# A message pass with one fp32 product per tile and a gather ring of 32 groups

## The chip, the cores and the metric

The kernel runs on one core of a Trainium2 chip. The time is the device time of one execution in microseconds; the figures below are the median of three runs and the times of one profiled execution. TensorE (PE) multiplies matrices, VectorE (DVE) and ScalarE (ACT) work on elements, GpSimd (POOL) issues the gathers, and SyncE (SP) issues loads and counts semaphores. All five run programs of their own and meet at semaphores.

## The reference

A graph of 6250 nodes with 96 features and 206,250 edges, sorted by destination. First a message layer, then three attention layers:

```python
def _mlp(h, W, b, gamma, beta):
    h = relu(h @ W + b)
    mu = mean(h, axis=0); var = mean(square(h - mu), axis=0)
    return gamma * (h - mu) * rsqrt(var + EPS) + beta

node_feat = _mlp(x, W_node, ...)                     # 6250 x 96
edge_feat = _mlp(edge_attr, W_edge, ...)             # 206250 x 4 -> 96
message = concatenate([x[row], x[col], edge_feat], axis=1)
message = _mlp(message, W_msg, ...)                  # 206250 x 288 -> 96
agg = segment_sum(message, col)
x = layernorm(x + agg + node_feat)
for l in range(3):                                   # 4 heads of 24
    h = x @ W[l]; e = leaky_relu(alpha_s[src] + alpha_d[dst])
    alpha = softmax of e over the edges of each dst
    x = relu(segment_sum(h[src] * alpha, dst) + bias[l])
x = layernorm(x0 + x)                                # x0: x before the attention
```

## The kernel before

The message product is split by the three parts of its input. `x @ W1` is computed once per node and written to a table in DRAM (`table_m`, 96 wide); the part of the source node is then one gathered row per edge. `x @ W2` belongs to the destination, and since the edges are sorted, a window of 32 destination nodes (`WA`) serves many edges. `edge_feat @ W3` is computed per edge, after the statistics of the edge features are known.

Edges come in 231 groups of 896 (`GE`), seven tiles (`TPG`) of 128. Where a group reaches over the border of a window it needs two steps; a list of steps in DRAM (`steps`), made by the kernel itself, says for each pair of steps which group, window and ring slot they take. The engines load a few values of that list into registers at the head of each pair.

The program goes through these stages, each a block with a barrier behind it:

1. Preparation: the edge attributes are split into bf16 parts and written to DRAM (`edge_parts`), the tables and the list of steps are made. VectorE splits `x @ W2` into three bf16 parts (`b_dram`), which are loaded again as `b_stack`.
2. Edge statistics: 403 chunks of 512 edges, TensorE (L592) to ScalarE's relu (L632) to VectorE's `bn_stats` (L677). GpSimd waits for the tables, clears memory and gathers the first two groups (L626), and then has nothing to do.
3. A small block that clears memory.
4. The message pass (`edge_block` with the class `Message`). It begins with the node products (TensorE L889, VectorE L898). Then each step runs, with lags of one and two steps: TensorE's `edge_product` (L1013: twice `pick`, which lays the digits of the destinations out, and twice `We_b`, the edge features); VectorE's `match_turned` (L924, a 96 x 896 match of destinations against the window's nodes, and the window's rows of b, L930 and L933); ScalarE's `edge_relu` (L986); TensorE's `message_product` (seven times an fp32 product with `W3s`, L1029, and a bf16 product of the match with `b_win`, L1030, into the same sum); VectorE's `add_source` (L953 twice, which adds the gathered rows, and L962), ScalarE's `square` (L993), VectorE's `add_squares` (L917), TensorE's `node_sums` (L1038), VectorE's `accumulate` (L911) and `match` (L940, L944).
5. A closing stage for the sums of the message layer (from L1337 on), then three attention passes through the same `edge_block`, with `table_a`.

GpSimd's order of work is `gather`: for each group it waits until the group's indices are there, until a slot of the ring of eight is free (`freed`), and, from group 8 on, until TensorE has finished the edge product of the same number of steps (`steps_told`, here `u_ready`; L785). Then it issues seven gathers of 128 rows (L790). SyncE hands over: it waits for the loads of edges (`tell_edges`) and for the landing of a group's seven gathers (`hand_over`, L732) and raises the counts that the other engines wait for; `release` (L734) reads when a group's last step is done, waits for it, raises `freed` and loads the edges of the group that takes the slot.

## Time and profile before

| | |
|---|---|
| median of three runs | 10644.16 us (10643.23 to 10644.27) |
| profiled execution | 10621.61 us, span 10619.8 us |
| GpSimd busy | 6506.8 us, 61% of the span |
| TensorE busy | 6152.5 us, 58% |
| VectorE busy | 4582.6 us, 43% |
| ScalarE busy | 3539.3 us, 33% |
| gathers of the message pass (L790, `table_m`) | 1603, 1608.5 us busy, 905.2 us idle before them |
| gathers of the attention passes (L790, `table_a`) | 4851, 4797.2 us busy, 2646.5 us idle before them |

The profile is read from the program's stages to the single step. The busy times are averages over stages with different limits. Idle time is put down to what ended it: "remote" is a semaphore that SyncE, a DMA or another sequencer raised, "issue" is time in which the engine waited for nothing that the profile shows (loading registers counts here), and a name is the instruction that released it. PEclk is the granted clock of TensorE as a share of 2.4 GHz, so 0.50 is 1.2 GHz.

### The profile page before, as it was taken

To read this page: it belongs to the slowest core of one execution; us is meant where nothing else is said; L and a number is where in the kernel's file an instruction comes from. 1 tells how busy PE (TensorE), PEld (TensorE's weight loads), DVE (VectorE), ACT (ScalarE), POOL (GpSimd) and SP (SyncE) were. 2 spreads that over 40 slices of the span, in tenths; PEclk is the share of its full clock that TensorE was granted. 3 is DMA by queue.
4 is the path that set the end of the run, shared out by engine and by line. 5 is a ranking of instruction groups with operands and counts; after the bars stand their busy time and mean duration, and the time that the engine had idled before them with its cause. 6 is when DMAs were issued, how large, how long until landed. Compare 5 with 4: busy or idle time off the path is not lost. (4 is left out here: it accounts for less than half of the span.)

```text
span 10619.8 us, 135368 instructions
## 1 busy us (share of the span) xinstructions
PE 6152.5 (58%) x29838; PEld 5414.6 (51%) x29838; DVE 4582.6 (43%) x11874; ACT 3539.3 (33%) x7369; POOL 6506.8 (61%) x6535
## 2 busy tenths in 40 slices
PE   6777777777855555555545555555454555555553
PEld 2366666666644444444444444444444444444443
DVE  8644444444543333333343333333334333333335
ACT  5411111111133333333333333333333333333333
POOL 0166666666656666666656666666665666666665
PEclk6555555555566666666666666666666666666665
DMA  5111111111111111111111111111111111111111
GB/s 140 27 37 37 36 37 37 37 37 37 35 35 34 34 34 34 34 34 35 34 35 34 35 34 35 34 35 34 34 34 36 34 34 34 35 34 35 34 35 29
DMA packets 310442, 395.85 MB, mean 37 GB/s; under 512 B 196635, under 2 KB 204177, under 8 KB 308201
## 3 DMA queue, kind: packets, MB, share of 16 engines
q0 software_dynamic: 206976, 330.75, 15.3%
q1 hardware_dynamic: 101577, 61.83, 2.6%
q10 hardware_dynamic: 1840, 2.78, 0.1%
q14 instruction: 37, 0.30, 0.0%
q8 instruction: 12, 0.20, 0.0%
HBM read 368.10 MB, written 26.82 MB: 37 GB/s over the span
## 5 line engine op out<-in xcount | busy, mean ns | idle before, releaser
L790 POOL DMA_INDIRECT rows<-table_a,idx x4851 | 4797.2, 989 | 2646.5 <-issue 1608.0
L1241 PE MATMUL ps<-ident,work 128*128 128x128 f32 x4872 | 1182.2, 418 | 2613.5 <-issue 2534.5
L1241 PEld LDWEIGHTS ps<-ident,work 128*128 128x128 f32 x4872 | 948.7, 221 | 2700.8 <-issue 2600.7
L1258 PE MATMUL ps<-rows,work 128*128 x9744 | 1759.6, 351 | 943.3 <-ACT work L1190 756.7
L1258 PEld LDWEIGHTS ps<-rows,work 128*128 128x128 f32 x9744 | 1637.2, 261 | 1128.9 <-issue 1125.0
L790 POOL DMA_INDIRECT rows<-table_m,idx x1603 | 1608.5, 1003 | 905.2 <-issue 522.4
L1197 ACT ACTIVATE work<-work,small 128x896 f32<-128x896 f32 x696 | 725.0, 1042 | 3640.9 <-issue 2316.9
L1134 DVE SCALAR_TENSOR_TENSOR work<-dstf,big,select 128x224 f32 x696 | 314.4, 452 | 3163.7 <-SPq L732 1658.0
L1123 DVE CUSTOM_DVE_ANT_0 work<-work,ps 128x896 f32<-128x896 f32 x696 | 757.0, 1088 | 1229.7 <-issue 924.7
L1029 PE MATMUL ps<-W3s,work 97*128 97x96 f32 x3248 | 1015.7, 468 | 349.4 <-DVE work L953 318.6
L1029 PEld LDWEIGHTS ps<-W3s,work 97*128 97x128 f32 x3248 | 909.7, 330 | 522.2 <-issue 274.8
L1249 PE MATMUL ps<-ident,work 128*128 128x128 f32 x4872 | 1102.1, 398 | 102.2 <-issue 102.2
L1249 PEld LDWEIGHTS ps<-ident,work 128*128 128x128 f32 x4872 | 991.0, 219 | 105.2 <-issue 105.2
L1190 ACT ACTIVATE work<-ps 128x896 f32<-128x896 f32 x696 | 632.0, 908 | 924.0 <-issue 881.4
L993 ACT ACTIVATE work<-work 128x672 f32<-128x672 f32 x232 | 177.5, 765 | 1900.6 <-DVE work L917 1252.2
L1144 DVE TENSOR_TENSOR work<-work,rows 128x896 f32<-128x896 f32 x696 | 761.1, 1093 | 99.2
L1183 ACT ACTIVATE work<-ps,small 128x896 f32<-128x896 f32 x696 | 687.2, 987 | 28.6 <-PE ps L1249 28.6
L1038 PE MATMUL ps<-work 128*97 128x32 f32 x3248 | 571.1, 348 | 5.7 <-issue 5.7
L1038 PEld LDWEIGHTS ps<-work 128*97 128x97 f32 x3248 | 558.6, 285 | 4.3 <-issue 3.5
L953 DVE TENSOR_TENSOR work<-ps,rows 128x384 f32<-128x384 f32 x464 | 220.7, 504 | 612.1 <-remote 538.0
L924 DVE TENSOR_SCALAR work<-ps,base_w,select 96x896 bf16<-96x896 f32 x232 | 279.7, 1206 | 454.1 <-issue 419.4
L1030 PE MATMUL ps<-work 96*128 96x96 bf16 x1624 | 464.9, 286 | 1.0 <-issue 1.0
(256 smaller groups left out, 6042.6 us busy)
## 6 DMA issues: line engine op xcount, KB each, us to landing
rows<-table_a,idx POOLq DMA_INDIRECT x4851
rows<-table_m,idx POOLq DMA_INDIRECT x1617
big<-edge_parts SPq DMA_DIRECT2D x231, 45.5 KB
edge_parts<-big SPq DMA_DIRECT2D x6, 1617.0 KB, 11.7
work<-edge_parts SPq DMA_DIRECT2D x50, 192.0 KB
table_a<-work SPq DMA_DIRECT2D x12, 606.0 KB, 6.4
b_dram<-big SPq DMA_DIRECT2D x3, 1176.0 KB, 8.2
big<-b_dram SPq DMA_DIRECT2D x3, 1176.0 KB
```

What stands on the lines that cost most here:

```text
L790: pool.indirect_dma_start(rows[:, k % RING, j, 0:width], None, table, bass.IndirectOffsetOnAxis(ap=idx[:, k // CHUNK, at:at + 1], axis=0)) ...
L1029: pe.matmul(o, ut[:, j, :], W3s[:], start=True, stop=False)
L1030: last = pe.matmul(o, match[:, j, :], b_win[:, par], start=False, stop=True)
L1038: last = pe.matmul(ps[0:MW, 6 + par, 0:WA], rr[:, par, j, :], eq[:, par, j, :], start=(j == 0), stop=(j == TPG - 1))
L1123: dve.tensor_tensor_reduce(out=logit[:, par], in0=logit[:, par], in1=ps[:, 2 * par:2 * par + 2, :].rearrange("p b n -> p (b n)")[:, 0:GE], ...
L1144: dve.tensor_tensor(masked[:, par], pen.unsqueeze(2).broadcast_to([P, TPG, H, WA]), source, ALU.add).then_inc(s["a_ready"], 1)
L1183: nc.scalar.activation(logit[:, par], ps[:, 2 * par:2 * par + 2, :].rearrange("p b n -> p (b n)")[:, 0:GE], ACT.Relu, bias=alone[:, par:pa ...
L1190: nc.scalar.activation(probT[:, par].rearrange("p j n -> p (j n)"), ps[:, 4:6, :].rearrange("p b n -> p (b n)")[:, 0:GE], ACT.Copy).then_i ...
L1197: nc.scalar.activation(prob[:, par].rearrange("p j e -> p (j e)"), logit[:, par], ACT.Exp, bias=shift[:, par:par + 1]).then_inc(s["p_ready ...
L1241: last = pe.transpose(ps[:, 4 + j // 4, (j % 4) * P:(j % 4 + 1) * P], prob[:, par, j, :], ident[:])
L1249: last = pe.transpose(ps[:, 2 * par + j // 4, (j % 4) * P:(j % 4 + 1) * P], masked[:, par, j].rearrange("p h n -> p (h n)"), ident[:])
L1258: last = pe.matmul(ps[:, 6 + par, 0:D + 1], probT[:, par, j, :], rows_of(at("slot", 3))[:, j, 0:D + 1], start=(j == 0), stop=(j == TPG - 1))
```

## The change

The message pass moves into the block of the edge statistics, and its ring has 32 groups of its own layout (`store`, 7 x 96 columns a group). GpSimd starts to gather when `table_m` is written, 32 groups straight away, beside the edge statistics; from then on a group waits for a free slot, for its indices, and for the landing of the group 16 before it, and no longer for TensorE. The semaphore count `begun` goes, in the attention passes too.

The message product becomes one fp32 product per tile, of depth 128: rows 0 to 95 are the relu of the edge features, rows 96 to 127 the match of the destinations against the 32 nodes of the window, and the weights are `W3` scaled, over the window's 32 rows of b. So `pick` and `We_b` become one matrix `We_dst` of 128 columns (two matmuls instead of four, in banks that alternate), the match is 32 x 896, and the bf16 parts of b with their split, their two window operations and the products L1030 go. The rows of b (`table_b`, fp32 in DRAM) and the edges are loaded by ScalarE, two DMAs per step, two steps ahead. The sums are kept in `XT`, cleared by VectorE before the first step. VectorE reads three quads of the list instead of four, TensorE none instead of one, ScalarE one instead of none. SyncE first issues the chunk loads of the edge statistics and then goes through its `hand_over` and `release`.

```diff
 RING = 8
-ERING = RING
+RING_M = 32
+TOLD_M = 16
+IDX_M = 4
 LAG = 4
-LEAD_M = 0
+LAG_M = 28
...
             @block.gpsimd
             def _(pool):
-                pool.wait_ge(s_tab, 16)
-                pool.wait_ge(shared["idx0"], 16)
-                pool.wait_ge(s_sent_b, 16 * 3)
-                pool.memset(acc_m[:, ESTAT:], 0.0)
-                for g in range(AHEAD):
+                def gather(g, k, turn):
+                    if k % CHUNK == 0:
+                        pool.wait_ge(s_midx[k // CHUNK], turn * 16 + 16)
+                    if not (isinstance(turn, int) and turn == 0 and k < TOLD_M):
+                        pool.wait_ge(shared[f"gat{k % TOLD_M}"], (turn * (RING_M // TOLD_M) + k // TOLD_M) * (16 * TPG))
+                        pool.sem_inc(shared["paced"], 1)
+                    for j in range(TPG):
+                        at = k % CHUNK * TPG + j
+                        pool.indirect_dma_start(store[:, (k * TPG + j) * D:(k * TPG + j + 1) * D], None, table_m,
+                                                bass.IndirectOffsetOnAxis(ap=idx[:, k // CHUNK, at:at + 1], axis=0)).then_inc(shared[f"gat{k % TOLD_M}"], 16)
+
+                pool.wait_ge(s_tab, 16)
+                for g in range(RING_M):
+                    if g == 8:
+                        pool.wait_ge(s_parts, 16 * (len(PARTS) + 2))
+                    if g == 12:
+                        pool.wait_ge(s_tab_b, 16 * 2)
+                    gather(g, g, 0)
+                def gather_later(i, k):
+                    pool.wait_ge(shared["freed"], i * RING_M + (k - (RING_M - 1)))
+                    gather(None, k, i)
...
-                        if not (isinstance(g, int) and g < emit.paced_from):
-                            pool.wait_ge(emit.steps_told, g - emit.lead)
-                            pool.sem_inc(paced, 1)
-                        pool.sem_inc(begun, 1)
...
+                def edge_product(q, par):
+                    pe.wait_ge(s_edges[par], q * 8 + (16 - 8 * par))
+                    if not (isinstance(q, int) and q < 2):
+                        pe.wait_ge(s["ut_ready"], q - 1)
+                        pe.wait_ge(s["eqt_ready"], q - 1)
+                    for half in range(2):
+                        last = pe.matmul(bank(2 * par + half, P, GE // 2), wt["We_dst"][:],
+                                         edges_in[:, par, half * (GE // 2):(half + 1) * (GE // 2)], start=True, stop=True)
+                    last.then_inc(s["u_ready"], 1)
...
+                        for j in range(j0, j1):
+                            last = pe.matmul(ps[:, 4 + half, (j - j0) * D:(j - j0 + 1) * D], both_parts[:, j, :], weights[:, par],
+                                             start=True, stop=True)
...
-                    dve.tensor_scalar(eqT[:, par].rearrange("p (b n) -> p b n", b=2), ps[0:3 * WA, 0:2, 0:GE // 2],
+                    dve.tensor_scalar(uT[D:, par].rearrange("p (b n) -> p b n", b=2), ps[D:, 2 * par:2 * par + 2, 0:GE // 2],
...
+                    dve.wait_ge(s_bin[par], q * 8 + (16 - 8 * par))
+                    dve.tensor_tensor(weights[D:, par], b_in[:, par], bias_b, ALU.add).then_inc(s["win_ready"], 1)
...
+                def step(q, par, live, at):
+                    if live(0):
+                        edge_relu(q, par)
+                    if live(-2):
+                        load_edges(par, at("edges", -2))
+                    if live(1):
+                        square(q - 1, (par - 1) % 2)
+                    if live(-2):
+                        act.wait_ge(s["win_ready"], q + 1)
+                        load_b(par, at("node", -2))
...
+                for g in range(LAG_M):
+                    hand_over(g % TOLD_M, g // TOLD_M)
+                    if g % CHUNK == CHUNK - 1:
+                        load_indices(g // CHUNK + IDX_M, g // CHUNK)
+                LOOPS = (NG - LAG_M - RING_M) // RING_M
+                with sp.Fori(0, LOOPS) as i:
+                    for u in range(RING_M):
+                        k = LAG_M + u
+                        hand_over(k % TOLD_M, i * (RING_M // TOLD_M) + k // TOLD_M)
+                        if k % CHUNK == CHUNK - 1:
+                            load_indices(i * IDX_M + k // CHUNK + IDX_M, k // CHUNK % IDX_M)
+                        release(sp, i * RING_M + u)
...
+                dve.memset(XT[:], 0.0).then_inc(s_clear, 1)
```

The order of GpSimd's instructions at the start of the message gathers, before. `big` is the memory of the sums, `rows` the ring.

```order
L622 MEMSET big 97x3872 [waits s_sent_b,idx0,s_tab]
L626 DMA rows<-table_m,idx 128x96 x14
L553 UNCONDITIONAL_BRANCH
L1051 UNCONDITIONAL_BRANCH [waits barrier_Pool_Activation_PE_DVE_SP_gather]
L1053 MEMSET big 97x2432
L1050 UNCONDITIONAL_BRANCH
L777 UNCONDITIONAL_BRANCH [waits barrier_Pool_Activation_PE_DVE_SP_gather]
L790 DMA rows<-table_m,idx 128x96 x42
L790 DMA rows<-table_m,idx 128x96 [waits u_ready,idx1,freed]
L790 DMA rows<-table_m,idx 128x96 x6
L790 DMA rows<-table_m,idx 128x96 [waits freed,u_ready]
```

The same place now; `store` holds the ring.

```order
L766 UNCONDITIONAL_BRANCH [waits barrier_Pool_Activation_PE_DVE_SP_gather]
L776 DMA store<-table_m,idx 128x96 [waits s_midx0,s_tab]
L776 DMA store<-table_m,idx 128x96 x55
L776 DMA store<-table_m,idx 128x96 [waits s_midx1,s_parts]
L776 DMA store<-table_m,idx 128x96 x27
L776 DMA store<-table_m,idx 128x96 [waits s_tab_b]
L776 DMA store<-table_m,idx 128x96 x27
L776 DMA store<-table_m,idx 128x96 [waits s_midx2,gat0]
L776 DMA store<-table_m,idx 128x96 x6
L776 DMA store<-table_m,idx 128x96 [waits gat1]
```

Two barriers stood between the first fourteen gathers and the rest, and `u_ready` before each group from the ninth on; now 224 gathers follow one barrier, with waits for landings (`gat`) alone from the seventeenth group on.

TensorE, the beginning of a step in the loop of the message pass, before; the pair of L1029 and L1030 stands seven times there, and seven L1038 follow.

```order
L1009 REGISTER_ALU [waits edged]
L1013 ISA [waits eqt_ready,ut_ready]
L1013 MATMUL ps<-big,pick 96x448
L1013 ISA
L1013 MATMUL ps<-big,pick 96x448
L1013 MATMUL ps<-big,sWe_b 96x448 x2
L1024 REGISTER_ALU [waits win_ready,ut_ready,eqt_ready]
L1029 MATMUL ps<-W3s,work 128x96 [waits v_ready]
L1030 MATMUL ps<-work 128x96
```

TensorE, a whole step in the loop now.

```order
L848 REGISTER_ALU [waits s_edges0]
L851 MATMUL ps<-work,sWe_dst 128x448 [waits eqt_ready,ut_ready]
L851 MATMUL ps<-work,sWe_dst 128x448
L865 MATMUL ps<-work 128x96 [waits win_ready,v_ready,ut_ready,eqt_ready]
L865 MATMUL ps<-work 128x96 x6
L872 REGISTER_ALU [waits rr_ready]
L874 MATMUL ps<-work 97x32 [waits done]
L874 MATMUL ps<-work 97x32 x6
```

A step had 4 + 14 + 7 matmuls and has 2 + 7 + 7; the wait for the edges is now one for ScalarE's load of them.

ScalarE, the first step of a pair, now. Before, there were its two ACTIVATE alone and no load of the list.

```order
L546 TENSOR_LOAD steps
L927 ISA
L929 ISA [waits u_ready]
L930 ACTIVATE work<-ps,cols 96x896 [waits pre_ready]
L915 REGISTER_ALU
L915 DMA work<-edge_parts 26x896
L936 REGISTER_ALU [waits rr_ready]
L937 ACTIVATE work<-work 128x672 [waits squares_added]
L918 ISA [waits win_ready]
L918 DMA work<-table_b 32x96
```

The load of b's rows stands behind the wait for `win_ready`, which VectorE raises when it has added the rows of this step, so behind it the next step's relu waits too.

## Rows read from the trace of the kernel before

**Rows 1.** Groups by line, 1000 to 2000 us: busy us, mean ns, idle before, releasers.

```profile
L790 POOL DMA_INDIRECT rows<-table_m,idx x654 | 655.1, 1002 | 346.6 <-issue 206.7 <-remote 119.9 <-PE ps L1013 20.0
...
L953 DVE TENSOR_TENSOR work<-ps,rows 128x288 f32<-128x288 f32 (+1 forms) x187 | 88.6, 504 | 243.7 <-remote 212.7 <-issue 17.0 <-PE ps L1030 7.5
```

**Rows 2.** Windows: length, then busy us (instructions) of each engine, PEclk, DMA share, GB/s.

```profile
200.00:370.00 170.00, 170.00 (x288) 42.56 (x287) 170.00 (x288) 170.00 (x287) 0.00 (x0) 0.50 0.15 40
403.00:448.00 45.00, 9.24 (x38) 8.03 (x37) 2.22 (x4) 0.00 (x0) 34.03 (x37) 0.50 0.19 40
1000.00:2000.00 1000.00, 786.44 (x3654) 676.40 (x3654) 485.30 (x939) 158.71 (x188) 654.88 (x654) 0.50 0.17 37
```

**Rows 3.** Timeline of GpSimd, 1490 to 1530 us: start, us, operation, idle before.

```profile
1495.26 0.94 POOL L790 DMA_INDIRECT rows<-table_m,idx  x1 [2.82 <-remote]
...
1516.37 1.22 POOL L790 DMA_INDIRECT rows<-table_m,idx  x1 [3.48 <-remote]
```

**Rows 4.** Timeline of TensorE, 1500 to 1512 us.

```profile
1500.90 0.97 PE L1013 MATMUL ps<-big,pick 26*96 x2 [4.12 <-DVE work L924]
...
1502.55 0.78 PE L1029 MATMUL ps<-W3s,work 97*128 97x96 f32 x2
...
1506.81 2.46 PE L1038 MATMUL ps<-work 128*97 128x32 f32 x14
```

**Rows 5.** Timeline of GpSimd, 120 to 142 us.

```profile
123.55 1.16 POOL L626 DMA_INDIRECT rows<-table_m,idx  x1 [0.17 <-issue]
...
139.98 0.94 POOL L626 DMA_INDIRECT rows<-table_m,idx  x1 [0.30 <-issue]
```

**Rows 6.** Timeline of VectorE, 128 to 147 us.

```profile
137.88 0.69 DVE L677 BATCH_NORM_STATS2 big<-work 96x512 f32 x1 [1.46 <-issue]
140.68 0.69 DVE L677 BATCH_NORM_STATS2 big<-work 96x512 f32 x1 [2.11 <-issue]
```

**Rows 7.** Timeline of VectorE, 376 to 472 us.

```profile
377.94 11.07 DVE L683 BATCH_NORM_AGGREGATE small<-big 96x2 f32<-96x2418 f32 x1
...
391.47 0.26 DVE L698 COPY node_fix<-ps 97x96 f32<-97x96 f32 x1
...
420.95 0.56 DVE L898 TENSOR_TENSOR xn<-xn,ps 128x384 f32<-128x384 f32 x1 [11.44 <-remote]
442.65 0.56 DVE L898 TENSOR_TENSOR xn<-xn,ps 128x384 f32<-128x384 f32 x1 [21.14 <-remote]
...
457.93 0.55 DVE L898 TENSOR_TENSOR xn<-xn,ps 128x384 f32<-128x384 f32 x1 [1.65 <-PE ps L889]
...
468.16 1.21 DVE L924 TENSOR_SCALAR work<-ps,base_w,select 96x896 bf16<-96x896 f32 x1 [6.10 <-issue]
```

**Rows 8.** Timeline of VectorE, 2903 to 2928 us.

```profile
2905.50 1.21 DVE L924 TENSOR_SCALAR work<-ps,base_w,select 96x896 bf16<-96x896 f32 x1 [3.81 <-issue]
2906.63 0.23 DVE L930 TENSOR_SCALAR work<-big,select 96x96 bf16 x1
2907.04 0.32 DVE L933 SCALAR_TENSOR_TENSOR work<-big,select,work 96x96 bf16<-96x96 bf16 x1 [0.18 <-issue]
...
2910.99 1.21 DVE L924 TENSOR_SCALAR work<-ps,base_w,select 96x896 bf16<-96x896 f32 x1
...
2926.57 0.19 DVE L911 TENSOR_TENSOR big<-big,ps 97x32 f32 x1 [0.61 <-PE ps L1038]
```

**Rows 9.** Timeline of TensorE, 5020 to 5035 us (attention).

```profile
5024.64 3.30 PE L1258 MATMUL ps<-rows,work 128*128 x14 [2.52 <-ACT work L1190]
```

**Rows 10.** Timeline of VectorE, 92 to 122 us.

```profile
92.87 2.61 DVE L165 CAST big<-xn 128x4704 bf16<-128x4704 f32 x1 [1.61 <-DMA steps<-work]
...
108.35 2.61 DVE L165 CAST big<-xn 128x4704 bf16<-128x4704 f32 x1
```

**Rows 11.** Groups by line of the whole run.

```profile
L362 DVE MEMSET XT<- 1x6272 f32 x1 | 5.3, 5285 | 1.3 <-issue 1.3
```

**Rows 12.** Timeline of GpSimd, 5003 to 5030 us (attention).

```profile
5005.79 1.51 POOL L790 DMA_INDIRECT rows<-table_a,idx  x1 [3.45 <-remote]
```

669 lines of the change are left out of this document (319 added, 350 removed).

## The prediction

> **What bounds the kernel now.** I read the page first, then the message stage in the view of its groups by line, its windows, and at last the timelines of single stretches. The message stage runs from about 462 to 2927 us of the span, the three attention passes behind it take the rest, and the change leaves their work alone except for one semaphore count. In the message stage the groups by line say that no engine is full: between 1000 and 2000 us GpSimd is busy 655 us with 654 gathers, TensorE 786, VectorE 485 [rows 1, 2]. The reader is to see what ends the waits. A gather costs 655.1 us busy and 206.7 us of "issue" over 654, so 1.318 us each and 9.22 us for a group of seven; 231 groups are 2130 us. The stage takes 232 steps from the first turned match at 468.16 to the last sum at 2926.57, 10.60 us each [rows 7, 8]. So GpSimd is nearest to the bound, and 1.4 us of each step is a pause in its stream.
>
> What ends the pause? VectorE's additions of the gathered rows wait 212.7 us in 1000 us for "remote", and GpSimd 119.9 us for "remote" [rows 1]. The timeline shows a stream that starts at 1495.26, fourteen gathers at 1.25 us, and then nothing for 3.48 us before the next at 1516.37 [rows 3]. Two places say what happens: hand-offs of TensorE come late while gathers stream without a gap. In the node product VectorE's additions of 0.56 us come after waits of 11.44 and 21.14 us for "remote" while 37 gathers stream between 403 and 448, and of 1.65 us behind that stream [rows 2, 7]. In the edge statistics the first fourteen gathers run from 123.55 to 139.98, and at 137.88 and 140.68 VectorE takes one chunk per 2.8 us [rows 5, 6], where 288 chunks take 170 us (0.59 each) without gathers [rows 2]. So the first ten us or so of a stream cost nothing, and then each hand-off is late until the stream has drained, some 3 us. In the message stage this makes two groups (17.5 us) plus 3.5 us of pause, or 10.5 us a group, which is the pace measured. The Trainium skill ("Trainium Architecture — The Big Picture", What this means for kernel authors) says that engine lanes and DMA ports of SBUF cannot contend, and that only VectorE and GpSimd share a port pair. By that rule a gather could not delay TensorE's hand-off, which is the first rival; the 21.14 us speak against it, though they do not say which path is shared.
>
> **The change part by part.** All times are those of the profiled execution, 10621.61 us for a span of 10619.8; the median of the runs shown is 10644.16, 22.6 above it, and I add the differences to the median.
>
> *TensorE per step.* Before: edge products from 1500.90 to 1502.55, 1.65; message products to 1506.81, 4.26; node sums 2.46: 8.4 us [rows 4]. After: two edge products instead of four (0.97) and seven fp32 products of depth 128 and width 96. The nearest row is attention's: fourteen rows (seven such products of 97 columns) in 3.30 us at 1.2 GHz [rows 9], which is also the granted clock of the message stage (0.50, [rows 2]). Sum 0.97 + 3.30 + 2.46 = 6.7 us, 1.7 less. Bounds: the products at 4.26 as now (7.7), or at half of 3.30 if 2.4 GHz were granted (5.1 and less).
>
> *VectorE per step.* An unstalled step runs 2905.50 to 2910.99, 5.49 us [rows 8]. The two window operations go (2906.63 to 2907.36 with their gap, 0.73), an addition of 32 x 96 comes (0.2, from the 0.19 of the 97 x 32 sum): 4.95. At each pair it reads its list, four quads for 3.81 us of "issue" [rows 8], now three: 2.9, or 1.4 per step. So 6.4. The Trainium skill ("Runtime: NRT & Kernel Launch", Instruction fetch mechanics) prices a register load at about 200 ns, so an estimate of 16 x 0.2 = 3.2 now and 2.4 after; trace and page agree roughly and the sum takes the row. TensorE and VectorE wait for each other once a step, so I take 7.3 us for an unstalled step, 6.7 and 8.0 as bounds. ScalarE gets a list read and four DMA issues per pair; it is busy 158.71 us in 94 steps now, 1.7 each [rows 2], so they are covered, as long as the loads land within the two steps that they have.
>
> *GpSimd.* Its gathers are as many and as long. They start when the table is written, not after the edge statistics. In the first block three casts and two subtractions (92.87 to 110.96, [rows 10]) go, 18 us; I take 13, since other engines work there too. The block then ends near 98, and gathers begin at about 103, once their indices have come (now 123.55, behind a memset and b's parts, which go). Then 32 groups at 8.85 us (13 intervals between 123.55 and 139.98 are 1.264 each) end at 386.
>
> *The edge statistics pay for it.* They begin near 108, and from 115 on until the stream drains at 389 they lie in the late regime: 274 / 2.8 = 98 chunks, about 10 before. The other 295 at 0.59 take 174: end at 563 instead of 377.9, 185 later. Bounds: no delay at all (end at 364), and the late regime of the node product, where 11 to 21 us per hand-off would leave 25 chunks done by 389, end at 612. I take 2.8 since it is the same work, but it was seen for three chunks only.
>
> *To the first step.* Aggregate and weights take 14 us as now (377.94 to 391.73, [rows 7]). The node additions, 13, now come with no gathers beside them and seven banks ahead: 8 us, where 408 to 457 alone were some 50. The memset of the 97 x 6304 sums is new in VectorE's row (5.3 by the 1 x 6272 one, taken to cost by columns, [rows 11]), list and barrier 4. First match at 563 + 14 + 8 + 5 + 4 = 594, against 468.16: **126 us later**.
>
> *The steps.* The ring is full by then, so GpSimd gathers what is freed: 231 - 32 = 199 groups. With no pacing, streams last as long as slots are free. In the first ten us of a stream the consumer does 10 / 7.3 = 1.4 steps and frees as many slots, so the stream goes on for one or two groups more, then lateness holds the steps up, no slot comes, the stream drains and a pause of 3.5 us follows. At n groups per stream the step takes 8.85 + 3.5 / n: 10.6 for 2, 10.0 for 3. I take 10.3. The last 32 steps have no gathers beside them: 7.3 each. End: 594 + 200 x 10.3 + 32 x 7.3 = 2888, against 2926.57: **39 us earlier**.
>
> *Behind it.* Closing: GpSimd's two memsets, the second after the sums, become one ahead of them, and small row memsets: -6 (0 to -11). Attention: one semaphore count less per group; it streams 14 gathers with 3.45 us of pause, as the row shows [rows 12], and the pause is ended by "remote", so 0 to -28 (0.04 us x 693 groups), I take -10. Sum: 126 - 165 - 16 = **-55 us, 10,590**.
>
> **The rivals.**
> 1. *Nothing is late, gathers are the bound* (0.08). For it: most additions of rows in the message stage wait for nothing but their product, and 32 groups of depth let a late hand-off pass unless the ring runs empty. Against: lateness holds the steps themselves up, as the 21.14 us show. Edge stage over at 364, first step at 400, 199 groups at 9.22 from there and two steps: 2250, 676 less, with the 16 behind it 9,950. This is also what the Trainium skill's rule on the two sides of SBUF (above) would make of it.
> 2. *One of the two stages is late, not both* (0.18). If only the edge stage: 594 + 199 x 9.22 + 10 = 2439, so 10,140. If only the steps: 400 + 2060 + 234 = 2694, so 10,396. For it: the edge stage's 2.8 us were seen in three chunks beside the writes of the first block; the steps have slack in the ring that the node product had not.
> 3. *Slower: what frees a slot is the end of a late chain* (0.32). Now GpSimd goes on when TensorE has begun a step (one hand-off behind the drain). After, it needs the sums of a step: product, addition, sums, SyncE's read and count. The pause is then 3.5 plus half a step, 3.6, so 7.1; if every second stream ends so, the step takes 8.85 + (3.5 + 7.1) / 4 = 11.5: 200 x 1.2 = +240, 10,830. If all do, 12.4 and 11,010. The point from which it decides is 10.57 us per step (594 + 200 c + 234 - 16 = 2926.57 gives c = 10.57); everything above is slower than before. Against it: a step freed early in a stream leaves a slot in hand, so GpSimd rarely waits for the newest.
> 4. *The edge stage is held up more* (in the forecast's range): 49 us later at 612, 10,640, and then no change.
>
> **How the numbers follow.** Forecast 0.42, first rival 0.08, second 0.18, third 0.32. The forecast alone spans 10,480 to 10,650 (10.0 to 10.6 a step, start 563 to 640). A measurement of this kernel tells 0.2% (21 us) from no change. The forecast's 0.42 divides into 0.32 faster, 0.08 same and 0.02 slower; with 0.26 of the first two rivals faster is 0.58, with 0.32 of the third slower is 0.34. The range for 8 in 10: from 10,100 (leaving out the case where nothing is late) to 10,850 (leaving out 12.4 a step).
>
> **What would show it.** Right: the edge statistics end between 540 and 610, with VectorE's chunks 2 to 3 us apart until the 224th gather and 0.6 behind it; node additions with no gap over 3 us; TensorE's step near 6.7 busy; GpSimd in streams of 14 to 28 gathers with pauses of 3 to 4 us ended by "freed"; the last 32 steps at 7 to 7.5. Wrong: chunks at 0.6 beside gathers (rival 1), pauses of 7 us and more (rival 3), waits of TensorE for the edge or b loads, which I priced at nothing.

## The result, and the profile after

The changed kernel takes 10,822.89 us (median of 4 runs, 10,764.87 to 10,858.72) against 10,643.69 for the kernel before: 1.0163 times as long, 95% interval 1.0118 to 1.0208, 179 us slower. The forecast was 10,590, so its sign was wrong; the time lies in its range, and the third rival had given 10,830. The profiled run is the slowest of the four, 10,858.72 us with a span of 10,856.9. The kernel before repeats to 1 us in that series, the changed one spreads over 94 us, and a later series of it gave 10,719.8 (experiment 5).

The profile's lines that answer to [rows 1, 8] and the table before:

```profile
PE 5791.6 (53%) x27752; PEld 5105.0 (47%) x27752; DVE 4498.6 (41%) x11640; ACT 3551.3 (33%) x7369; POOL 6485.7 (60%) x6545
...
L776 POOL DMA_INDIRECT store<-table_m,idx x1617 | 1566.3, 969 | 1369.3 <-SPq L580 787.0
...
L865 PE MATMUL ps<-work 128*128 128x96 f32 x3248 | 817.7, 443 | 981.3 <-DVE work L1053 868.3
...
L1053 DVE TENSOR_TENSOR work<-ps,store 128x384 f32<-128x384 f32 x464 | 223.2, 504 | 929.0 <-remote 879.9
```

Every engine is busy for less time than before, and the kernel is slower. GpSimd now waits 787 us for SyncE's L580, the line that frees a slot (253 of them for the first slot, from the 32nd group to 656), and VectorE's additions wait 880 us for "remote". The stages of the two profiled executions, from their timelines:

| | before | after | difference grows by |
|---|---|---|---|
| first gather | 123.55 | 114.49 | |
| statistics aggregated from | 377.94 | 611.27 | +233 |
| first step's match | 468.16 | 642.43 | -59 |
| last sum | 2926.57 | 3146.25 | +45 |
| first gather of the attention | 2995.30 | 3225.35 | +10 |
| end of the span | 10619.8 | 10856.9 | +7 |

The windows of the changed kernel, as [rows 2]: busy us (instructions) of TensorE, its weight loads, VectorE, ScalarE, GpSimd, then the clock.

```profile
160.00:360.00 200.00, 37.36 (x57) 8.44 (x57) 39.34 (x57) 38.91 (x57) 150.59 (x158) 0.50 0.22 46
440.00:600.00 160.00, 160.00 (x271) 40.17 (x270) 160.00 (x271) 160.00 (x271) 0.00 (x0) 0.50 0.16 42
1000.00:2000.00 1000.00, 565.88 (x2588) 492.08 (x2587) 415.63 (x775) 147.19 (x172) 586.32 (x608) 0.50 0.17 35
2960.00:3140.00 180.00, 176.24 (x815) 155.10 (x815) 130.87 (x248) 46.88 (x55) 0.00 (x0) 0.50 0.04 8
```

VectorE's operations are no longer for it (L1053, 128 x 384, takes 0.56 us with and without gathers); what is late is their beginning. Beside gathers the edge statistics take 57 chunks in 200 us, 3.5 us each; without them 271 in 160, 0.59 each. The steps go at 1000 / 86 = 11.6 us beside gathers (775 VectorE instructions, nine a step) and at 6.6 us without them, behind 2936, when TensorE is busy for 176 of 180 us. (The row from 2960 lies behind the last gather.)

The cycle of the steps on three engines. First GpSimd, as [rows 3]: a stream of fourteen, then 5.5 us.

```profile
1496.53 0.94 POOL L776 DMA_INDIRECT store<-table_m,idx  x1 [5.47 <-SPq L580]
...
1513.31 0.95 POOL L776 DMA_INDIRECT store<-table_m,idx  x1 [0.30 <-issue]
1519.79 0.94 POOL L776 DMA_INDIRECT store<-table_m,idx  x1 [5.53 <-SPq L580]
```

TensorE in that cycle, as [rows 4]:

```profile
1502.61 3.51 PE L865 MATMUL ps<-work 128*128 128x96 f32 x14 [1.84 <-issue]
1505.92 2.39 PE L874 MATMUL ps<-work 128*97 128x32 f32 x14
1508.24 0.92 PE L851 MATMUL ps<-work,sWe_dst 26*128 26x448 bf16 x2
1517.45 2.85 PE L865 MATMUL ps<-work 128*128 128x96 f32 x11 [8.29 <-DVE work L1053]
```

VectorE in that cycle, as [rows 8]:

```profile
1508.85 0.56 DVE L1053 TENSOR_TENSOR work<-ps,store 128x384 f32<-128x384 f32 x1 [2.33 <-remote]
1516.73 0.46 DVE L1053 TENSOR_TENSOR work<-ps,store 128x288 f32<-128x288 f32 x1 [7.32 <-remote]
1517.22 0.86 DVE L1062 SCALAR_TENSOR_TENSOR work<-work,small 128x672 f32<-128x672 f32 x1
1517.99 0.85 DVE L1024 TENSOR_TENSOR work<-work 128x672 f32<-128x672 f32 x1
1518.76 0.18 DVE L1018 TENSOR_TENSOR XT<-XT,ps 97x32 f32 x1
```

TensorE's product ends by 1506.1 in the model of the profile, and VectorE adds its second half at 1516.73, 2.5 us after the last gather of the stream ended (1514.26). Then come the rest of that step (to 1518.94, 2.2 us) and SyncE's release (0.85), and only then a slot. These three make the 5.5 us. The loads that ScalarE now issues are not in this chain: between 1000 and 2000 us neither TensorE's edge products (the row below, no idle time before them) nor VectorE's additions of b (L1035) waited for one.

```profile
L851 PE MATMUL ps<-work,sWe_dst 26*128 26x448 bf16 x174 | 80.2, 562 | 0.0
```

The first step and the aggregation, as [rows 7]:

```profile
611.27 11.06 DVE L983 BATCH_NORM_AGGREGATE small<-store 96x2 f32<-96x2418 f32 x1
...
637.09 5.31 DVE L1007 MEMSET XT<- 97x6304 f32 x1 [1.26 <-issue]
642.43 1.22 DVE L1031 TENSOR_SCALAR work<-ps,base_w,pshift 32x896 f32<-32x896 f32 x1
```

The attention passes stream fourteen gathers with 3.40 us of pause, as [rows 12].

### The profile page after: what moved, and what is told of

It reads as the page before. It is cut to its first block and busy times, and to the rows that moved or that the text cites. A ratio compares the mean times of both kernels' runs of the same rounds, so it can differ in the third digit from the quotient of the medians.

```text
span 10856.9 us, 129391 instructions
## 1 busy us (share of the span) xinstructions
PE 5791.6 (53%) x27752; PEld 5105.0 (47%) x27752; DVE 4498.6 (41%) x11640; ACT 3551.3 (33%) x7369; POOL 6485.7 (60%) x6545
## 5 line engine op out<-in xcount | busy, mean ns | idle before, releaser
L635 POOL DMA_INDIRECT store<-table_a,idx x4851 | 4830.9, 996 | 2615.2 <-issue 1610.2
L776 POOL DMA_INDIRECT store<-table_m,idx x1617 | 1566.3, 969 | 1369.3 <-SPq L580 787.0
L1274 PE MATMUL ps<-store,work 128*128 x9744 | 1767.5, 352 | 955.3 <-ACT work L1206 633.4
L1274 PEld LDWEIGHTS ps<-store,work 128*128 128x128 f32 x9744 | 1637.0, 261 | 1150.8 <-issue 1148.8
L1150 DVE SCALAR_TENSOR_TENSOR work<-dstf,store,select 128x224 f32 x696 | 314.0, 451 | 3153.3 <-SPq L598 1645.6
L865 PE MATMUL ps<-work 128*128 128x96 f32 x3248 | 817.7, 443 | 981.3 <-DVE work L1053 868.3
L865 PEld LDWEIGHTS ps<-work 128*128 128x128 f32 x3248 | 765.5, 324 | 1161.5 <-issue 1155.2
L1160 DVE TENSOR_TENSOR work<-work,store 128x896 f32<-128x896 f32 x696 | 761.0, 1093 | 99.2
L1053 DVE TENSOR_TENSOR work<-ps,store 128x384 f32<-128x384 f32 x464 | 223.2, 504 | 929.0 <-remote 879.9
L1031 DVE TENSOR_SCALAR work<-ps,base_w,pshift 32x896 f32<-32x896 f32 x232 | 283.6, 1222 | 396.7 <-issue 345.7
L1220 ACT ACTIVATE work<-ps,select 128x97 f32<-128x97 f32 x1392 | 390.6, 333 | 67.5 <-remote 36.8
```

The source lines that it names most:

```text
L635: pool.indirect_dma_start(rows[:, k % RING, j, 0:width], None, table, bass.IndirectOffsetOnAxis(ap=idx[:, k // CHUNK, at:at + 1], axis=0)) ...
L776: pool.indirect_dma_start(store[:, (k * TPG + j) * D:(k * TPG + j + 1) * D], None, table_m, bass.IndirectOffsetOnAxis(ap=idx[:, k // CHUNK ...
L865: last = pe.matmul(ps[:, 4 + half, (j - j0) * D:(j - j0 + 1) * D], both_parts[:, j, :], weights[:, par], start=True, stop=True)
L1160: dve.tensor_tensor(masked[:, par], pen.unsqueeze(2).broadcast_to([P, TPG, H, WA]), source, ALU.add).then_inc(s["a_ready"], 1)
L1274: last = pe.matmul(ps[:, 6 + par, 0:D + 1], probT[:, par, j, :], rows_of(at("slot", 3))[:, j, 0:D + 1], start=(j == 0), stop=(j == TPG - 1))
```

## The experiments

All are edits of the changed kernel, and each time is given as a ratio to the kernel before, run in turn on the same chip, since the kernel before itself lay between 10,602 and 10,647 us from series to series.

**1. A step's beginning ends the pause.**

```diff
                     pool.wait_ge(shared["freed"], i * RING_M + (k - (RING_M - 1)))
+                    pool.wait_ge(m_sems["u_ready"], i * RING_M + (k - 20))
```

> The changed kernel, but from the 33rd group on GpSimd also waits until TensorE has begun the step 20 before the group, so that it is a step's beginning and no longer a freed slot that ends a pause. Theory A (the pause is 5.5 us because a slot comes free only behind the whole late step and SyncE's release): pauses of about 3.5 us as before, 10.5 us a step instead of 11.6, the total about 200 us below the changed kernel, 10,620. Theory B (it is the step itself, with ScalarE's loads, that is slow beside gathers): pauses and total as in the changed kernel, 10,820.

Measured 10,584.38 us, ratio 0.9989 (0.9979 to 0.9998). Pauses are 2.97 us in the mean. GpSimd's timeline in this run, the first gather of each of three streams:

```profile
1502.05 0.94 POOL L776 DMA_INDIRECT store<-table_m,idx  x1 [2.86 <-remote]
...
1522.82 0.94 POOL L776 DMA_INDIRECT store<-table_m,idx  x1 [3.04 <-remote]
...
1543.57 0.94 POOL L776 DMA_INDIRECT store<-table_m,idx  x1 [2.23 <-PE ps L852]
```

Two groups take a cycle of 20.8 us instead of 23.3, as theory A had it, though the start is as late as before (634 us). How much of this the new wait did is another matter. The next two experiments ran in the same series, keep the changed kernel's rule in the steps, and have pauses of 3.6 and 3.3 us in the mean, not 5.5. Experiment 5 shows why: under that rule pauses come in two lengths. What the new wait does is to leave out the long one: here and in experiments 9 and 11, which wait for a step's beginning too, none of 285 pauses is above 4.2 us.

**2. No gathers before the steps.**

```diff
                 pool.wait_ge(s_tab, 16)
+                pool.wait_ge(s_node_added, NB)
```

> The changed kernel, but GpSimd begins to gather only when the node additions are done. Theory A (gathers hold up the edge statistics): one chunk per 0.6 us throughout, first step at about 415 us instead of 642. The ring is empty then and GpSimd streams without a wait for 32 groups, in which the steps should be at their slowest; behind that 11.6 us a step. If the steps behind it cost as much as before, the total is 10,770 or so (405 + 231 x 11.6). Theory B (edge statistics are slow for another reason, the wider weights or SyncE's loads): still about 3 us a chunk, first step above 600.

Measured 10,701.16, ratio 1.0085 (1.0068 to 1.0102). Its windows beside the edge statistics, and behind the start of the gathers at 392.9:

```profile
120.00:340.00 220.00, 212.75 (x365) 54.72 (x365) 212.92 (x364) 213.47 (x361) 0.00 (x0) 0.50 0.19 51
```

```profile
400.00:700.00 300.00, 38.29 (x160) 34.57 (x160) 24.06 (x43) 8.83 (x10) 228.28 (x233) 0.50 0.19 40
```

Chunks take 0.60 us and the first step comes at 398.6: the edge statistics are slow for the gathers alone. The second row is the late state at its worst: 43 VectorE instructions, five steps, in 300 us, while GpSimd streams 32 groups without a wait (until 681). The total is 69 us below the 10,770 of theory A, since the pauses behind that are 3.6 us and not 5.5.

**3. A landing between the first 32 groups.**

```diff
+                    if g and g % 1 == 0:
+                        pool.wait_ge(shared[f"gat{(g - 1) % TOLD_M}"], ((g - 1) // TOLD_M + 1) * (16 * TPG))
                     gather(g, g, 0)
```

> The changed kernel, but each of the first 32 groups waits until the group before it has landed, so that no stream beside the edge statistics is longer than seven gathers (8.8 us). Theory A (only what lies more than some ten us into a stream is late): chunks at 0.6 us, first step at about 415 us, 24 groups or more in the ring by then, total about 220 us below the changed kernel, 10,600. Theory C (gathers slow the hand-offs in proportion to their share, wherever they stand in the stream): the edge statistics stay slow for longer, since the 32 groups now take 350 us, and the first step comes after 650.

Measured 10,422.99, ratio 0.9843 (0.9821 to 0.9864). Groups take 10.3 to 10.8 us, and 322 chunks fit into 120 to 340 us (0.68 each); the first step comes at 428.7. The delay of the edge statistics is gone, and the kernel is 1.6% faster than the one before. It is also 180 us below theory A's 10,600, which counted the earlier start alone: the steps, too, take 10.6 us here and not 11.6. That it is the length of a stream which decides does not follow, as the next run shows.

**4. A map of patterns.**

```diff
...
+                    if g in (4, 5, 6, 7, 8, 10, 12, 16, 20):
+                        drained(g)
+                    if g in (8, 12, 16, 20):
+                        rest(6)
+                    if 13 <= g < 16:
+                        rest(5)
+                    if 20 < g < 24:
+                        rest(2)
+                    gather(g, g, 0, rest if 16 <= g < 20 else None)
+                    if g == 23:
+                        rest(70)
```

`drained` waits for the group before to land, `rest(n)` is n memsets of 128 x 256, one waiting for the other, 0.36 us each.

> The changed kernel with a map of patterns for the first 32 groups beside the edge statistics, read by the spacing of VectorE's chunks: groups 0 to 3 without a pause, 4 to 7 each behind the landing of the one before, 8 to 11 in pairs behind a landing, 12 to 15 with a few us of GpSimd's own memsets between groups but no wait for a landing, 16 to 19 with a short memset after every gather, 20 to 23 with under a us of memsets between groups, then some 30 us of memsets alone, then groups 24 to 31 without a pause. Theory A (a backlog builds up in a stream and is gone some 3 us after it): late after ten us in 0 to 3, 8 to 11 late at their ends, 4 to 7 and 12 to 15 at 0.6 us a chunk, memsets alone at 0.6, and 16 to 19 less late than 0 to 3 if the backlog is one of rate. Theory D (GpSimd's being busy as such delays the others): memsets alone are late too.

One run, 10,580.22 us. Windows over the groups 4 to 7, 12 to 15, the memsets alone, and 25 on:

```profile
145.00:183.00 38.00, 7.87 (x13) 1.79 (x13) 8.97 (x13) 8.88 (x13) 24.90 (x27) 0.50 0.19 44
227.00:264.00 37.00, 33.67 (x58) 8.48 (x57) 34.71 (x59) 34.04 (x59) 28.83 (x42) 0.50 0.29 70
350.00:376.00 26.00, 22.06 (x38) 5.65 (x38) 23.11 (x40) 22.82 (x39) 21.92 (x69) 0.50 0.13 34
388.00:440.00 52.00, 10.50 (x16) 2.39 (x16) 10.53 (x16) 10.93 (x16) 39.44 (x42) 0.50 0.21 47
```

Memsets alone are harmless (40 chunks in 26 us), so theory D falls. Groups 4 to 7 had a pause of 1.8 us each, behind a landing, and stayed late (2.9 us a chunk), since they began late; groups 12 to 15 with 2.0 us, and no wait for a landing, stayed prompt (0.63), having begun prompt. Groups 16 to 19, a gather each 1.45 us, went from 0.60 to 0.92. So it is the rate that counts, and what went before: per gather the prompt groups took 1.49 us and the late ones 1.47 or less. I call this a debt, which fast gathers run up and a pause pays; that is a picture and not shown. In its simplest form it does not come out: at 1.48 us each the first 28 gathers, 1.25 us apart, would owe 6.4 us, yet group 8 was prompt after group 7 had taken 12.35 us with its pause, which pays 2.0. Nothing of a debt is seen in the landings, which came 1.8 us behind the last issue even after 28 gathers in a row.

**5. The changed kernel again.** 

> The changed kernel itself again, beside the runs that it is compared with: 10,765 to 10,860 as in its first four runs, or lower if its pauses depend on the chip; in the runs before this one, kernels with the same rule showed pauses of 3.3 to 3.75 us instead of 5.5.

Measured 10,719.8 (10,700.35 to 10,778.51), ratio 1.0068 (1.0051 to 1.0084). Its pauses are 4.4 us in the mean, its steps take 10.97 us beside gathers, and the first step is at 634.8. The mean hides what happens: nearly all pauses up to 1213 us are of 5.7 us, most of those from 1235 to 2266 are of 3.1 to 3.5, and behind that they are of 5.7 again. The change from one to the other, as [rows 3]:

```profile
1213.29 0.95 POOL L776 DMA_INDIRECT store<-table_m,idx  x1 [5.71 <-SPq L580]
...
1234.64 0.95 POOL L776 DMA_INDIRECT store<-table_m,idx  x1 [3.14 <-SPq L580]
```

Both end with the same release. In a short one VectorE's second addition comes before the stream is over (at 1611.78, the stream ends at 1613.94) and only the sums behind it (L1018, at 1616.14); in a long one the addition itself comes 2.5 us behind the stream. In the first profile 90 of 94 pauses were long (4.7 us or more), here 45 of 98, in experiments 2 and 3 only 17 of 93 and 9 of 92. So the changed kernel's time depends on how many of its streams fall into the long pattern; what tips it from one to the other is open.

**6. Five memsets behind every group of the message pass.**

```diff
+        def pause(pool, first=False):
+            if not first:
+                pool.wait_ge(s_junk, 5)
+                pool.sem_clear(s_junk)
+            for n in range(5):
+                if n:
+                    pool.wait_ge(s_junk, n)
+                pool.memset(junk[:], 0.0).then_inc(s_junk, 1)
...
                     for j in range(TPG):
...
+                    pause(pool)
```

> The changed kernel, but behind every group of the message pass GpSimd does five short memsets (1.8 us) of its own, so that a group takes 10.4 us instead of 8.75. Theory A2 (something takes about 1.47 us per gather while GpSimd issues one per 1.25 us, and hand-offs are late once the backlog has grown to some ten gathers): nothing is ever late; edge statistics at 0.65 us a chunk, first step at about 430 us, 231 groups at 10.4 to 10.5 us from 106 on, so the pass ends at about 2530 instead of 2927, the total is 10,200 to 10,250. Theory C (gathers hold the others up whenever they stream, and it is pauses with nothing in flight that help): the memsets are lost time, 10.6 us a step or more beside a late start, 10,650 or above.

Measured 10,415.9, ratio 0.9786 (0.9770 to 0.9803): 300 us less than the changed kernel of the same series, by doing more. The first step is at 442.3, no step is left at the end, and VectorE's additions no longer wait for TensorE's hand-offs but for landings. It is 165 us or more above what theory A2 gave for it, because a group took 11.2 us in the steps, where I had put 10.4: besides the 1.8 us of memsets there are waits at their ends and for slots, and some gathers take 1.3 us and more in place of 0.94.

**7. The same in the attention too,** in `edge_block`'s `gather`:

```diff
                         for j in range(TPG):
...
+                        pause(pool)
```

> As the run before, and the same five memsets behind every group of the attention passes too. Theory A2: the attention passes, at 10.63 us a step with 14 gathers and 3.4 us of pause, are at their bound of 7 x 1.47 = 10.3 but for the pauses, so they gain up to 0.2 us a step or 140 us in 693 groups, total about 10,080. If attention's steps are held by their own work, no gain or a loss of some 10 us.

Measured 10,898.0, ratio 1.0237 (1.0220 to 1.0254). A miss: from its first gather of the attention on it takes 8110 us, 479 more than the changed kernel's 7631. GpSimd's window holds 1057 instructions, 88 groups of twelve in 1000 us, 11.35 us each, and its rows show that it waited for nobody: the 142.8 us of "remote" that it waits in this window in the kernel before are gone, and 2.1 us for a slot are all that is left. So the memsets took the place of the pauses and are longer than they were; attention steps of 10.6 us were then held up by GpSimd itself. Fewer memsets there were not tried.

```profile
4000.00:5000.00 1000.00, 511.19 (x2465) 468.96 (x2466) 359.68 (x1061) 354.81 (x795) 760.87 (x1057) 0.61 0.16 32
```

```profile
L647 POOL DMA_INDIRECT store<-table_a,idx x617 | 622.3, 1009 | 218.5 <-issue 216.5 <-SPq L581 2.1
L592 POOL MEMSET junk<- 128x256 f32 x440 | 139.0, 316 | 20.2
```

**8. Other transfers in place of the gathers.**

```diff
+                        to = store[0:lanes, (k * TPG + j) * D:(k * TPG + j) * D + width]
+                        if plain:
+                            pool.dma_start(to, table_m[j * P:(j + 1) * P, :]).then_inc(shared[f"gat{k % TOLD_M}"], 16)
+                            continue
...
+                    if 5 <= g < 10:
+                        gather(g, g, 0, lanes=64)
+                    elif 10 <= g < 15:
+                        gather(g, g, 0, width=D // 2)
+                    elif 15 <= g < 20:
+                        gather(g, g, 0, plain=True)
+                    elif 20 <= g < 25:
+                        gather(g, g, 0, lanes=32)
```

> The changed kernel with other transfers in place of the gathers of the first 25 groups, so the message sums are of other data: groups 0 to 4 as they are (128 rows of 384 bytes), 5 to 9 with 64 rows, 10 to 14 with 128 rows of 192 bytes, 15 to 19 with 128 plain rows of 384 bytes without indices, 20 to 24 with 32 rows, then as they are; each kind begins after a pause of some 5 us. The spacing of VectorE's chunks tells the cost: if the backlog is one of rows (descriptors), 64 and 32 rows are never late and 192 bytes are late as before; if it is one of bytes, 64 rows and 192 bytes are both prompt; if it comes from GpSimd's work on an indexed gather, the plain rows are prompt; if it is the count of transfers, all kinds are late alike.

One run, 10,813.75. Windows over 64 rows, 192 bytes, plain rows, and 32 rows:

```profile
165.00:205.00 40.00, 7.88 (x12) 1.79 (x12) 8.25 (x12) 8.20 (x12) 29.84 (x33) 0.50 0.13 25
225.00:260.00 35.00, 8.29 (x13) 1.78 (x12) 7.78 (x12) 7.88 (x12) 26.25 (x28) 0.50 0.17 31
264.00:284.00 20.00, 17.53 (x30) 4.48 (x30) 19.02 (x32) 18.29 (x31) 18.53 (x35) 0.50 0.44 116
296.00:328.00 32.00, 6.56 (x10) 1.49 (x10) 5.80 (x10) 7.10 (x11) 23.77 (x28) 0.50 0.09 17
```

Half and a quarter of the rows, and half of the bytes, are as late as whole gathers (3 us a chunk). Plain transfers of the same rows and bytes, issued at more than twice the rate, are not (32 chunks in 20 us). So neither the number of rows nor that of bytes decides.

**9. The rule of the kernel before.**

```diff
                     pool.wait_ge(shared["freed"], i * RING_M + (k - (RING_M - 1)))
+                    pool.wait_ge(m_sems["u_ready"], i * RING_M + (k - 0))
```

> The changed kernel, but from the 33rd group on GpSimd also waits until TensorE has begun as many steps as there are groups before it, which is the rule of the kernel before. The start stays late (about 635 us, groups 1 to 32 unchanged). Theory A (the pause is as long as the chain that ends it): pauses of about 2.5 us in streams of 7 and 14 as before, 10.5 us a step for 199 steps; the first 32 steps after the start need no gathers from this rule and run at 6.7, and no step is left over at the end, so 635 + 32 x 6.7 + 199 x 10.5 = 2940, total about 10,650, level with before. Theory B (the new product or its loads make a step beside gathers slow): 11 us a step or more, total above 10,750.

Measured 10,670.39, ratio 1.0030 (1.0018 to 1.0042). Pauses 3.25 us, first step 634.8, last match 2956.0. As theory A had it, 20 us above its number: with the old rule the late start and the shorter product cancel.

**10. Three memsets,** as experiment 6 but

```diff
-            for n in range(5):
+            for n in range(3):
```

> As the run with five memsets behind every group of the message pass, with three (1.1 us), so that a group can take 9.7 to 9.9 us, 1.40 per gather. Theory A2 (about 1.47 us of something per gather): late again once a backlog has grown, in the edge statistics above 2 us a chunk for most groups, and the gain of the five memsets over the changed kernel mostly gone: 10,550 to 10,650. Theory E (any break of more than a us at each seventh gather ends the late state or keeps it away): chunks as with five memsets, and GpSimd 0.7 us a group faster: 10,270.

Measured 10,442.67, ratio 0.9824 (0.9807 to 0.9840). Between the theories: a group takes 9.7 to 9.9 us beside the edge statistics, and these are late all along, as A2 said.

```profile
120.00:340.00 220.00, 65.02 (x102) 15.03 (x101) 65.64 (x98) 66.49 (x100) 167.48 (x222) 0.50 0.25 57
```

98 chunks in 220 us where five memsets gave 293. But the steps, starting at 611.4 only, made up for it: GpSimd took 10.5 us a group and hardly ever waited for a slot, and 232 steps went at 9.11.

**11. Five memsets in the first 32 groups, then the wait of experiment 1.**

```diff
                     gather(g, g, 0)
+                    pause(pool)
...
+                    pool.wait_ge(m_sems["u_ready"], i * RING_M + (k - 20))
```

> Five memsets behind each of the first 32 groups only, and from the 33rd on the wait for TensorE's step 20 before. If the two delays add (edge statistics, and the pause in the steps): first step at about 440, steps as in the run with that wait alone (199 groups at 10.7, the last 22 steps at 6.4): end of the pass at 2710, total 10,420 against 10,640 for the kernel before. If the one depends on the other, within 50 us of the better of the two alone.

Measured 10,471.45, ratio 0.9852 (0.9836 to 0.9869). First step 437.1, last match 2749.4, 50 us above what adding the two gave; steps 10.33 us where experiment 1 had 10.19.

**12. Four memsets everywhere and the wait of experiment 1.**

```diff
-            for n in range(5):
+            for n in range(4):
...
+                    pool.wait_ge(m_sems["u_ready"], i * RING_M + (k - 20))
```

> Four memsets (1.45 us) behind every group of the message pass, and the wait for TensorE's step 20 before. Theory A2: 10.2 us a group is 1.46 per gather, just at the bound: edge statistics about 0.9 us a chunk, 10.4 a step, total 10,300 to 10,400. Theory E: as with five memsets but 0.35 us a group faster, 10,340.

Measured 10,486.72, ratio 0.9862 (0.9846 to 0.9879). Groups of 10.0 to 10.3 us lie in the middle: 168 chunks in 220 us, 1.3 each, and the first step at 552.6. Both theories had put the total lower, at 10,300 to 10,400 and at 10,340.

```profile
120.00:340.00 220.00, 104.81 (x169) 25.31 (x169) 106.34 (x168) 107.53 (x166) 171.01 (x241) 0.50 0.27 63
```

**13. Five memsets, then three.**

```diff
+                    n = 5 if isinstance(turn, int) and turn == 0 else 3
+                    pause(pool, rested[-1], n)
```

> The changed kernel with five memsets of GpSimd behind each of the first 32 groups and three behind each later one. Theory F (each stage has its own optimum: beside the edge statistics the gathers must stay below one per 1.47 us, since these are held up by each late hand-off; in the steps GpSimd only must not stop for a slot, and 32 groups of lead pay for slower steps): first step at 440, 199 groups at 10.57 from there, end of the pass at 2550, total 10,310. If the steps need the prompt state, the ring fills up and GpSimd waits for slots again: 10,400 or more.

Measured 10,285.16 (10,273.58 to 10,299.11), ratio 0.9667 (0.9651 to 0.9683): 350 us faster than the kernel before, the fastest here, and 25 us from its forecast. First step 445.4, last match 2566.8, GpSimd 10.6 us a group and almost never a wait for a slot. That the steps bear late hand-offs, as theory F says, is not shown by it: in the steps a group with three memsets takes 10.6 us, 1.51 per gather, where beside the edge statistics it takes 9.9 (experiment 10), since some gathers now take 1.1 to 1.6 us in place of 0.94. So by the rate these steps are not in the late state.

```profile
1515.23 1.08 POOL L592 MEMSET junk<- 128x256 f32 x3
1516.84 0.95 POOL L788 DMA_INDIRECT store<-table_m,idx  x1 [0.53 <-issue]
```

**14. Five memsets, then two.**

```diff
-                    n = 5 if isinstance(turn, int) and turn == 0 else 3
+                    n = 5 if isinstance(turn, int) and turn == 0 else 2
```

> The same with two memsets behind each later group. By theory F GpSimd's group takes 10.1 us and the total is 10,230 if 32 groups of lead suffice for steps of about 9 us; if steps in the late state take more than 10.1 us, slots run out and it is level with the three memsets or slower.

Measured 10,477.29, ratio 0.9850 (0.9834 to 0.9866). One memset less per group costs 192 us: steps beside gathers take 10.46 us instead of 9.18, the ring fills, GpSimd waits for slots, and 30 steps remain when it is done. So with two memsets the steps are slower than GpSimd, with three they are not.

**15. Plain transfers only, for long.**

```diff
                 for g in range(RING_M):
+                    gather(g, g, 0, plain=g < 24)
```

> The changed kernel with plain transfers of 128 rows of 384 bytes by GpSimd, without indices, in place of the gathers of the first 24 groups (so the sums are of other data): 168 of them, some 90 us in one stream, then eight groups of gathers. If only indexed gathers bring the late state, VectorE's chunks stay at 0.6 us beside the plain ones throughout and go to 3 us some ten us into the gathers. If any transfer of GpSimd's does once the stream is long enough, chunks go to 2 us and more within the first 90 us.

One run, 10,583.29. Windows inside the plain stream, inside the gathers behind it, and behind both:

```profile
150.00:190.00 40.00, 40.00 (x70) 10.19 (x69) 40.00 (x69) 40.00 (x70) 40.00 (x77) 0.50 0.52 137
217.00:265.00 48.00, 9.84 (x15) 2.25 (x15) 9.65 (x14) 10.42 (x16) 36.12 (x40) 0.50 0.22 47
290.00:390.00 100.00, 100.00 (x169) 25.09 (x168) 100.00 (x170) 100.00 (x170) 0.00 (x0) 0.50 0.15 42
```

168 plain transfers in 89 us leave the chunks at 0.58 us; gathers bring them to 3.4 within ten us. It is the indexed form.

## Why the prediction was wrong

**What bounds the kernel** was read rightly: hand-offs late beside a stream of gathers. The reading that "the first ten us or so of a stream cost nothing" described the symptom. What the runs show is a rate, in the edge statistics: beside groups of 10.4 us and more (1.49 per gather) chunks take 0.65 to 0.75 us, at 10.0 to 10.3 they take 1.3, at 9.8 they take 2.2, and at 8.8, 3.5. A stream at 1.25 us per gather is late after ten gathers and a pause of 1.8 us in seven does not end the state once it is there (experiment 4). From these rows I estimate 10.3 to 10.4 us as the least that a group costs without holding anyone up; the 10.60 us a step of the kernel before and 10.63 in attention were already near it. The picture of two groups and a pause of 3.5 us was also taken from one place: between 500 and 2850 us the kernel before pauses 66 times behind fourteen gathers, 3.5 us in the mean, but 84 times behind seven, 1.7 us. The first rival, where nothing is late and a group takes 9.22, has no run for it.

**The edge statistics.** I put 2.8 us a chunk and the end at 563; it was 3.5 and 611. The three chunks of [rows 6] were the whole basis. The gathers began at 114.5, not 103: the 18 us of VectorE went, but in this execution TensorE took 20 us for the products of the tables that it did in 10 before (48 of them between 74 and 84 us instead of 92, at a granted clock of 1.00 in both), and ScalarE copied them at that pace, so the block ended at 111 as before. In the later profile of the same kernel they went at 92 and the first gather is at 106.8. Both together make the first step 48 us later than forecast, 642 for 594.

**An unstalled step.** Forecast 7.3 us with 6.7 and 8.0 as bounds; measured 6.6, between TensorE's sum of 6.7 and VectorE's 6.4. The product of depth 128 took 3.51 us where attention's row gave 3.30. This is just below the lower bound of 6.7, and worth only 20 us in the last 30 steps, because beside gathers the steps are held by late hand-offs and not by work.

**The step that failed** is the pause: "a pause of 3.5 us follows. At n groups per stream the step takes 8.85 + 3.5 / n ... I take 10.3." n was 2 in 94 of the 95 streams between 650 and 2850 us, and the pause 5.5 us, since what ends it is no longer the beginning of a step but its end and SyncE's release. That is the third rival, with its place and its size: it said 7.1 us in every second stream, 5.3 in the mean and 11.5 us a step; measured 5.5 in nearly every stream and 11.6. That its 10,830 lies 7 us from the median is luck in part: the profiled run is 237 us above the one before where the rival had 187, the first step is 48 us later than the rival had it too, and the series of experiment 5, where half of the pauses are of the short kind, is at 10,719.8. I had it at 0.32 on the ground that a step freed early leaves a slot in hand. It does not: the ring is full when the steps begin, and its depth is used up by the 30 steps that remain when GpSimd has finished (2936). A ring that is full gives no slack to its filler. Experiments 1, 9 and 11 take this one cause away, and the long pauses are gone. What it costs depends on how often the long pattern comes: experiment 1 is 1.7% below the changed kernel's first series and 0.8% below that of experiment 5, each against the kernel before in its own series.

**Behind the pass.** Closing was forecast at -6 and came at +10. GpSimd's one memset of 16.60 us now lies beside VectorE's short operations, where before one of 11.34 us did. The rows show VectorE's L1439 held until it ends:

```profile
3147.13 16.60 POOL L1488 MEMSET store<- 128x19800 f32 x1 [210.17 <-POOLq L712]
```

```profile
3154.88 8.90 DVE L1439 TENSOR_SCALAR lift<-ident,small 96x96 f32<-96x96 f32 x1
```

3154.88 + 8.90 is 3163.78, and the memset ends at 3163.73; in the kernel before the same operation took 4.28 us and ended with its memset too. That is 4.6 of the 10 us; the others lie behind L1439, and no run parts them. The Trainium skill ("SBUF — State Buffer", SBUF: two separate sides) has VectorE in a two-port mode and GpSimd share a port pair under an exclusive lock for a whole instruction. The trace agrees with this (8.90 us beside the memset), though no row shows in which mode L1439 ran. Attention was forecast at -10 and came at +7, so no gain from the count `begun` is seen.

The rule that engine lanes and DMA ports of SBUF cannot contend (the Trainium skill, "Trainium Architecture — The Big Picture", What this means for kernel authors) is not contradicted: rows and bytes did not matter (experiment 8). The conclusion I let it stand for, that gathers cannot delay hand-offs, is.

**What stays open** is which part of an indexed gather delays the others' hand-offs, and what tips the same kernel between pauses of 5.7 and of 3.3 us. ScalarE's loads were not waited for; whether its list read and its wait for `win_ready` cost anything beside gathers was not tried apart.

## What to carry to other kernels

When an engine off the critical path is let loose, ask first what its work does to the others' hand-offs: here the kernel with GpSimd let loose was 179 us slower in one series and 73 in another, and making it slower by 1.8 us a group beside the edge statistics and 1.1 beside the steps gained 350 us over the kernel before. A deep ring pays only while it is being emptied: fill it where the consumer isn't running, without slowing that stage, and set the filler's pace so that it never waits for a slot and the ring is empty at the end (experiment 13). Look at a pause over many streams and not at its mean alone, since one kernel can fall into two patterns. And price a wait by the whole chain behind its semaphore, not by the length of the wait that it replaces.

## What the runs showed of the hardware

- Indexed gathers by GpSimd, 128 rows of 384 bytes, issue every 1.25 us, but beside more than one per 1.47 to 1.49 us hand-offs between TensorE, ScalarE and VectorE were late in the edge statistics: a chunk of three instructions on four banks went from 0.59 to 3.5 us. With 32 or 64 rows, or 192 bytes, it is the same; with plain transfers, 168 in 89 us, it doesn't happen; with GpSimd's memsets neither.
- The late state has a memory: seven gathers in 10.26 us (1.8 us of pause) did not end it in three groups, a pause of 3.9 us after them did, and seven in 10.42 us, begun after such a pause, did not bring it back.
- At its worst, with gathers streaming for 289 us, five steps, which take 6.6 us each without gathers, took 300 us.
- With the slot rule the same kernel paused 5.7 us for 23 streams, then 3.3 for some 50, then 5.7 again, in one execution.
